# A four-layer fp32 model on one core: another order of the seven products of an expert slot, and the second ranking cut into ten parts

## The chip, the core and the metric

The kernel runs on one core of a Trainium2 chip. The core has TensorE (matrix products, PE in the profile), VectorE (DVE), ScalarE (ACT), GpSimd (POOL) and SyncE (SP, whose queue starts the loads). Each engine has its own program and runs it in order; the engines meet only in semaphores. The metric is the time of one execution on the device in microseconds.

## The reference, cut to what matters

Two layers, each a mixer and a feed-forward part with a residual and a layer norm behind it. 2048 tokens of width 512, everything in fp32. Layer 0 is a state-space mixer and a block-sparse feed-forward part, layer 1 is a linear attention and the mixture of experts in which the change lies:

```python
weights = _router_weights(x, Wr, temperature)          # sigmoid, exponentials, rank of 8 experts, top 2
gate = jnp.einsum('btd,edf->ebtf', x, Wg)               # 8 experts, 512 x 512
up = jnp.einsum('btd,edf->ebtf', x, Wu)
gate = gate.at[:NL].add(jnp.einsum('btd,edr,erf->ebtf', x, Ga, Gb))     # rank 64, 2 of the experts
up = up.at[:NL].add(jnp.einsum('btd,edr,erf->ebtf', x, Ua, Ub))
mid = jax.nn.silu(gate) * up
out = jnp.einsum('ebtf,efd->ebtd', mid, Wd)
out = out.at[:NL].add(jnp.einsum('ebtf,efr,erd->ebtd', mid[:NL], Da, Db))
return jnp.einsum('bte,ebtd->btd', weights, out)
```

## The kernel before

**Slots.** The experts' part runs in 32 slots. A slot is half an expert (256 of the 512 hidden columns) over half the tokens (1024); slots 0 to 15 take the first half of the tokens, 16 to 31 (`SLOTS` = 16) the second. Slots 18 to 29 are a loop, the others are written out. In a slot n TensorE makes the hidden sums of slot n (`up`) and, between them, the outputs of slot n-1 (`down`). fp32 products are made of three matmuls (`accumulate`, L1232: high x high, low x high, high x low), so every operand is there twice, as `_hi` (rounded, by ScalarE) and `_lo` (the rest, by VectorE or GpSimd).

**Seven products.** `up` doesn't make eight block products but seven of sums of blocks (Strassen's way in Winograd's form). Product q has an operand a[q] made of weights and b[q] made of tokens, and two halves i (gate and up), each of 6 matmuls of 512 columns. They go to three pairs of banks of PSUM: X (`attn_pvk`) takes q = 0, 2, 4, 6, one on top of the other, Y (`attn_pt`, `attn_pk`) takes q = 1, Z (`attn_po`) takes 3 and 5. Between them sums are read out: after q = 0 ScalarE copies X into c_t0 (`take`, semaphore s_e1) and VectorE adds Y to it (`combine`); after 2 and 4 ScalarE copies X again; after 3 and 5 VectorE adds Z. X after q = 6 is the last block (c_last): ScalarE takes silu of half 0 (L2300), VectorE multiplies half 1 by it (L2899). Only then may q = 0 of the next slot overwrite X: half 0 waits for the silu, half 1 for the product. q = 2 waits for the copies of s_e1.

**Down.** The eight `down` products c = 0 to 7 (6 matmuls each) go through a ring of two banks (`attn_pv`, `attn_pq`). VectorE adds each to `all_acc` with its router weight (`add_down`, L2762, in `turn`), which frees the bank. `downs(n)` places them: one after each of q = 0 to 3, two after 4, one after 5 and 6. Slots 3, 4, 7, 8 (`MERGING`) also put small matmuls of the rank-64 parts into the ring (L2478 to L2484; added by VectorE at L2773 and L2777), slot 10 (`TURNING`) transposes of the second half's tokens (L2493), slot 11 (`SCORING`) its router scores.

**Around it.** For slot n+1, ScalarE cuts a[q] (`up_high`) and VectorE makes the rest (`up_low`, L2720) while slot n runs; only q = 6 and the down weights (`down_high`, `down_low`, L2730) are made at the start of their own slot. GpSimd makes the sums of weights, the rest of the hidden values (`hidden_low`, L2020) and, in slot 15, four sums of tokens (`x_sums`, L2003 to L2013), from which b[q] of the second half is made: `x_high` on ScalarE, `x_low` (L2726) on VectorE, in slot 15 and at the start of slot 16. The ranking of the second half (`router(1, part)`) is in slot 12 (`RANKING`): part 0 after down product 0, 1 after 4, 2 after 6, 3 and 4 after 7, with two exponentials on ScalarE (`router_functions(1, 1)`) in front of the last silu. `side_work` calls them from `turn`. The weights that it makes are first used in slot 17. In slot 17 `finish` normalizes the first half's output.

The order within an engine is that in which `slot` of each engine is written; there is no scheduler.

## Time and profile before

| | us |
|---|---|
| median of 3 runs | 2319.34 (2316.86 to 2319.48) |
| the profiled execution | 2319.87, its span 2318.2 |
| TensorE busy in the span | 2257.0 |
| VectorE, ScalarE, GpSimd busy | 1582.3, 891.1, 766.6 |
| slots 0 to 31 | from about 1304 to 2300 of the span |

A row of busy time says how long an engine had an instruction in work; matmuls overlap, so their starts are the better measure. A row of the timeline ends in square brackets with the time the engine stood idle before it and the instruction whose end released it.

### The profile page before, as it was taken

The numbers are of one execution on the slowest core, as the hardware profiler recorded it, in microseconds if no ns is written. First come the engines' busy times: TensorE is split into PE (matmuls) and PEld (weight loads), VectorE is DVE, ScalarE is ACT, GpSimd is POOL, SyncE is SP. The second block draws the span as 40 slices with busy tenths as digits, with TensorE's granted clock in tenths as the row PEclk, the third lists the DMA queues.
The fourth block names the chain that finished last, engine by engine and source line by source line (L and its number), as shares of the span: only waits on it lengthen the run. The fifth ranks groups of instructions, "written<-read, shape, count | busy, mean of one in ns | idle before, by whom it ended". The sixth has DMA issues, their size and how long they took to land.

```text
span 2318.2 us, 30910 instructions
## 1 busy us (share of the span) xinstructions
PE 2257.0 (97%) x10746; PEld 1863.4 (80%) x10746; DVE 1582.3 (68%) x2394; ACT 891.1 (38%) x1455; POOL 766.6 (33%) x585
## 2 busy tenths in 40 slices
PE   8999999999999999999999899999999999999998
PEld 7887788888878888888877787878778778888886
DVE  5557777777778755683446776867677887666665
ACT  5456333333343222322232543534344444444443
POOL 0003544444413222342111523424233533333332
PEclk9999999999999999999999999999999999999999
DMA  6856222222150100000000122222011021111110
GB/s 210 230 153 185 64 73 72 72 72 72 55 200 15 37 19 19 23 1 19 1 1 28 64 73 91 73 82 82 28 55 55 28 91 55 54 54 54 54 36 37
DMA packets 93224, 155.95 MB, mean 67 GB/s; under 512 B 6576, under 2 KB 56752, under 8 KB 86848
## 3 DMA queue, kind: packets, MB, share of 16 engines
q1 hardware_dynamic: 93120, 154.59, 20.4%
q8 instruction: 61, 1.00, 0.2%
q14 instruction: 43, 0.35, 0.0%
HBM read 115.25 MB, written 39.32 MB: 67 GB/s over the span
## 4 chain that ended last, share of the span: by engine, by line
PE 62%; DVE 5%; issue 2%; ACT 1%; POOL 1%; DVEq 0%; POOLq 0%; ACTq 0%
PE attn_pvk L1235 4%; PE attn_pvk L1236 4%; PE attn_pvk L1237 4%; PE attn_pq L1235 2%; PE attn_pq L1236 2%; PE attn_pq L1237 2%; PE attn_po L1235 2%; PE attn_po L1236 2%; PE attn_po L1237 2%; PE attn_pv L1235 2%; PE attn_pv L1236 2%; PE attn_pv L1237 2%; PE attn_pv L85 2%; PE attn_pv L87 2%; PE attn_pv L86 2%
## 5 line engine op out<-in xcount | busy, mean ns | idle before, releaser
L2720 DVE TENSOR_TENSOR moe_a_lo<-moe_up_raw,moe_a_hi 128x512 fp32r<-128x512 f32 x192 | 183.3, 970 | 147.6 <-ACT moe_a_hi L2153 147.5
L2020 POOL TENSOR_TENSOR moe_h_lo<-moe_c_t,moe_h_hi 128x512 fp32r<-128x512 f32 x96 | 128.5, 1339 | 351.8 <-ACT moe_h_hi L2153 351.8
L1235 PE MATMUL attn_pvk<-moe_b_hi,moe_a_hi 128*128 128x512 f32 x512 | 201.5, 393 | 10.8 <-ACT moe_c_last L2300 7.0
L1237 PE MATMUL attn_pvk<-moe_b_hi,moe_a_lo 128*128 128x512 f32 x512 | 200.3, 391 | 0.0
L1236 PE MATMUL attn_pvk<-moe_b_lo,moe_a_hi 128*128 128x512 f32 x512 | 200.2, 391 | 0.0
L2153 ACT ACTIVATE moe_c_t<-attn_pvk 128x512 f32<-128x512 f32 x192 | 112.8, 595 | 175.9 <-PE attn_pvk L1237 174.1
L1349 POOL TENSOR_TENSOR ffn_h_lo<-ffn_h_f,ffn_h_hi 128x512 fp32r<-128x512 f32 x64 | 92.9, 1453 | 240.1 <-ACT ffn_h_hi L1416 240.1
L1593 DVE SCALAR_TENSOR_TENSOR all_acc<-attn_pvk,ffn_wts,all_acc 128x512 f32<-128x512 f32 x128 | 91.1, 749 | 93.3 <-PE attn_pvk L87 88.3
L2219 ACT ACTIVATE moe_c_t<-moe_c_t 128x512 f32<-128x512 f32 x96 | 60.4, 629 | 241.4 <-DVE moe_c_t L2802 241.3
L2153 ACT ACTIVATE moe_a_hi<-moe_up_raw 128x512 fp32r<-128x512 f32 x192 | 116.0, 624 | 56.4 <-POOL moe_up_raw L1990 56.4
L1235 PEld LDWEIGHTS attn_pvk<-moe_b_hi,moe_a_hi 128*128 128x128 f32 x512 | 96.6, 189 | 34.8 <-issue 8.9
L2762 DVE SCALAR_TENSOR_TENSOR all_acc<-attn_pv,moe_wts,all_acc 128x512 f32<-128x512 f32 x123 | 91.8, 746 | 37.7 <-PE attn_pv L1237 36.7
L1990 POOL TENSOR_TENSOR moe_up_raw<-moe_up_raw 128x512 f32<-128x512 f32 x32 | 52.0, 1624 | 188.2 <-DVE moe_a_lo L2720 188.1
L2802 DVE TENSOR_TENSOR moe_c_t<-moe_c_t,attn_po 128x512 f32<-128x512 f32 x128 | 86.3, 684 | 39.8 <-ACT moe_c_t L2153 36.5
L1178 DVE SCALAR_TENSOR_TENSOR mix_conv<-mix_acc,mix_cw,mix_conv 128x511 f32<-128x511 f32 (+2 forms) x96 | 71.8, 748 | 60.5 <-ACT mix_conv L686 58.2
L1237 PEld LDWEIGHTS attn_pvk<-moe_b_hi,moe_a_lo 128*128 128x128 f32 x512 | 96.7, 189 | 20.4
L2762 DVE SCALAR_TENSOR_TENSOR all_acc<-attn_pq,moe_wts,all_acc 128x512 f32<-128x512 f32 x133 | 99.1, 745 | 20.1 <-PE attn_pq L1237 17.1
L1236 PEld LDWEIGHTS attn_pvk<-moe_b_lo,moe_a_hi 128*128 128x128 f32 x512 | 96.7, 189 | 19.5
L1235 PE MATMUL attn_pq<-moe_dn_hi,moe_h_hi 128*128 128x512 f32 x266 | 105.5, 397 | 5.3 <-DVE all_acc L2762 4.0
L85 PE MATMUL mix_tp<-mix_wx_hi,mix_x 128*128 128x512 f32 x256 | 106.9, 417 | 0.0
L1235 PE MATMUL attn_po<-moe_b_hi,moe_a_hi 128*128 128x512 f32 x256 | 101.2, 395 | 4.0 <-DVE moe_c_t L2802 4.0
L85 PE MATMUL mix_acc<-mix_x_hi,mix_w_hi 128*128 128x512 f32 (+1 forms) x256 | 102.2, 399 | 1.7 <-DVE mix_x_lo L1153 0.9
(526 smaller groups left out, 6579.7 us busy)
## 6 DMA issues: line engine op xcount, KB each, us to landing
moe_up_raw<-in_e_up SPq DMA_DIRECT2D x28, 1024.0 KB, 6.1
moe_dn_raw<-in_e_dn SPq DMA_DIRECT2D x28, 512.0 KB, 3.7
xh<-mix_out_hi SPq DMA_DIRECT2D x32, 256.0 KB, 2.6
zs<-mix_out_z SPq DMA_DIRECT2D x32, 256.0 KB, 3.5
xl<-mix_out_lo SPq DMA_DIRECT2D x32, 256.0 KB, 3.9
mix_x<-xh SPq DMA_DIRECT2D x16, 512.0 KB, 4.1
mix_x<-xl SPq DMA_DIRECT2D x16, 512.0 KB, 5.2
mix_z_raw<-zs SPq DMA_DIRECT2D x16, 512.0 KB, 3.9
```

The source lines that it names most:

```text
L85: pe.matmul(out, lh, rh, start=first, stop=False)
L1178: nc.vector.scalar_tensor_tensor(out=conv[:, j % 2, d:SEQ], in0=acc[:, 2 * j % 4, 0:SEQ - d], scalar=cw[:, j, TAPS - 1 - d:TAPS - d], in1= ...
L1235: pe.matmul(out, lh, rh, start=first, stop=False, skip_group_check=True)
L1236: pe.matmul(out, lh, rl, start=False, stop=False, skip_group_check=True)
L1237: return pe.matmul(out, ll, rh, start=False, stop=True, skip_group_check=True)
L1349: nc.gpsimd.tensor_tensor(h_lo[:, f], h_f[:, f % 2], raw(h_hi[:, f]), ALU.subtract).then_inc(s_hlo, 1)
L1593: stt(out=acc[:, ch], in0=pd[c], scalar=wts[:, ch, bass.ds(F * u + f, 1)], in1=acc[:, ch], op0=ALU.mult, op1=ALU.add).then_inc(s_acc, 1)
L2020: tt(h_lo[:, m, tok], src, raw(h_hi[:, m, tok]), ALU.subtract).then_inc(s_hlo, 1)
L2153: copy = lambda out, src: nc.scalar.activation(out, src, ACT.Copy)
L2720: tt_(a_lo[q][:], src, raw(a_hi[q][:]), ALU.subtract).then_inc(s_alo, 1)
L2762: stt(out=acc[:, ch], in0=bank, scalar=wts[:, ch, w] if isinstance(w, slice) else wts[:, ch, bass.ds(w, 1)], in1=acc[:, ch], op0=ALU.mult, ...
L2802: tt_(c_t[tile][:, i], c_t[tile][:, i], bank(i), ALU.add).then_inc(sem, 1)
```

## The change

In every slot but slot 0 TensorE makes product 1 first and product 0 second; the down products keep their places (after the first, the second, and so on). `place_of` turns the waits on the count of products accordingly. ScalarE cuts a[6] and the down weights before it copies X for s_e1, where it did so after. The ranking of the second half is cut into ten parts: 0 and 1 stay in slot 12, 2 to 8 follow down products 1 to 7 of slot 13, part 9 down product 1 of slot 14; the two exponentials move to slot 13. The first half's ranking has the same instructions in the same order. Of the second half's token parts on VectorE, `x_low` 2 is made after the last product of slot 15 where 3 was, and 3, 5 and 6 within slot 16, after down products 0, 2 and 3. No instruction is added or removed.

```diff
+        TURN = (1, 0, 2, 3, 4, 5, 6)
...
+        place_of = lambda n, q: q if at(n, 0) else TURN[q]
...
-                reach(act, s_up, 14 * (n - 1) + 2 * q + 2)
+                reach(act, s_up, 14 * (n - 1) + 2 * place_of(n - 1, q) + 2)
...
-                    act.wait_ge(s_up, 14 * (SLOTS - 1) + 2 * q + 2)
+                    act.wait_ge(s_up, 14 * (SLOTS - 1) + 2 * place_of(SLOTS - 1, q) + 2)
...
-                act.wait_ge(s_up, 14 * n + 2 * q + i + 1)
+                act.wait_ge(s_up, 14 * n + 2 * place_of(n, q) + i + 1)
...
                     hidden_high(n - 1, (0, 1), used_by(n - 1, 7))
+                up_high(n, s, u, 6)
+                down_high(n, s)
                 if not at(n, 0):
                     take(n, 0, 0, s_e1, 0, 1)
                     take(n, 1, 0, s_e1, 0, 1)
+                lora_high(n, 0)
+                if at(n, SLOTS - 1):
+                    x_high(1, 0)
+                if at(n, RANKING + 1):
+                    router_functions(1, 1)
                 if at(n, SLOTS):
                     x_high(1, 5)
                     x_high(1, 6)
-                up_high(n, s, u, 6)
-                down_high(n, s)
-                lora_high(n, 0)
-                if at(n, SLOTS - 1):
-                    x_high(1, 0)
...
-                if at(n, RANKING):
-                    router_functions(1, 1)
...
-                for q in range(7):
+                for step in range(7):
+                    q = step if at(n, 0) else TURN[step]
                     for i in range(2):
                         if not (at(n, 0) and (q, i) in FIRST):
                             up(n, q, i)
-                    for c in downs(n)[q]:
+                    for c in downs(n)[step]:
                         extras(n, c)
...
                 if n == TOKENS_AT + 1:
-                    router(0, 2)
+                    for part in (2, 3, 4, 5):
+                        router(0, part)
                 if n == TOKENS_AT + 2:
-                    router(0, 3)
+                    router(0, 6)
+                    router(0, 7)
...
-                dve.wait_ge(s_up, 5 if at(n, 0) and (q, i) == (1, 1) else 14 * n + 2 * q + i + 1)
+                dve.wait_ge(s_up, 5 if at(n, 0) and (q, i) == (1, 1) else 14 * n + 2 * place_of(n, q) + i + 1)
...
-                    ranks(pr[:], cmp1, cmp2)
-                if part == 3:
+                if part in (2, 3, 4, 5):
+                    ranks(pr[:], cmp1, cmp2, part)
+                if part == 6:
                     link(red(sel[:], cmp1[:], AX_X, ALU.add))
                     ts(sel[:], sel[:], 1.5, None, ALU.is_lt).then_inc(s_router, 1)
                     dve.wait_ge(s_router, pair + 1)
                     link(tt_(sel[:], sel[:], pr[:], ALU.mult))
+                if part == 7:
                     inverse_of_sum(sel[:])
...
-                if at(n, RANKING):
-                    if c in (0, 4, 6, 7):
-                        router(1, {0: 0, 4: 1, 6: 2, 7: 3}[c])
-                    if c == 7:
-                        router(1, 4)
+                if at(n, RANKING) and c in (0, 4):
+                    router(1, c // 4)
+                if at(n, RANKING + 1) and c:
+                    router(1, c + 1)
+                if at(n, RANKING + 2) and c == 1:
+                    router(1, 9)
...
-                if at(n, SLOTS):
-                    x_low(1, 5)
-                    x_low(1, 6)
                 up_low(n, s, 6)
                 down_low(n, s)
                 turn(*order[0])
+                if at(n, SLOTS):
+                    x_low(1, 3)
...
                 turn(*order[2])
+                if at(n, SLOTS):
+                    x_low(1, 5)
...
                 turn(*order[3])
                 if more and not merging and not at(n, 0):
                     following(3)
+                if at(n, SLOTS):
+                    x_low(1, 6)
...
                 turn(*order[5])
-                if at(n, SLOTS - 1):
-                    x_low(1, 2)
...
                 if at(n, SLOTS - 1):
-                    x_low(1, 3)
+                    x_low(1, 2)
                 turn(*order[6])
```

TensorE at the seam of slots 15 and 16, the last three matmuls of down product 7 and the first three of slot 16. Before:

```order
L1235 MATMUL attn_pv<-moe_dn_hi_4439,moe_h_hi_4446 128x512
L1236 MATMUL attn_pv<-moe_dn_lo_4436,moe_h_hi_4446 128x512
L1237 MATMUL attn_pv<-moe_dn_hi_4439,moe_h_lo_4447 128x512
L1235 MATMUL attn_pvk<-moe_b_hi0_4422,moe_a_hi0_4415 128x512
L1236 MATMUL attn_pvk<-moe_b_lo0_4423,moe_a_hi0_4415 128x512
L1237 MATMUL attn_pvk<-moe_b_hi0_4422,moe_a_lo0_4461 128x512
```

Now:

```order
L1235 MATMUL attn_pv<-moe_dn_hi_4439,moe_h_hi_4446 128x512
L1236 MATMUL attn_pv<-moe_dn_lo_4436,moe_h_hi_4446 128x512
L1237 MATMUL attn_pv<-moe_dn_hi_4439,moe_h_lo_4447 128x512
L1235 MATMUL attn_pt<-moe_b_hi1_4424,moe_a_hi1_4416 128x512
L1236 MATMUL attn_pt<-moe_b_lo1_4425,moe_a_hi1_4416 128x512
L1237 MATMUL attn_pt<-moe_b_hi1_4424,moe_a_lo1_4462 128x512
```

The slot opens on the Y bank (`attn_pt`) with b[1], where it opened on X (`attn_pvk`) with b[0].

ScalarE at the start of slot 15 (every slot from 1 on has these rows; c_t2 and c_last are slot 14's hidden values). Before:

```order
L2153 ACTIVATE moe_h_hi_4446<-moe_c_t2_4448 128x512
L2153 ACTIVATE moe_h_hi_4446<-moe_c_last_4449 128x512
L2153 ACTIVATE moe_c_t0_4437<-attn_pvk 128x512 x2
L2153 ACTIVATE moe_a_hi6_4421<-moe_up_raw_4460 128x512
L2153 ACTIVATE moe_dn_hi_4439<-moe_dn_raw_4440 128x1024
```

Now:

```order
L2156 ACTIVATE moe_h_hi_4446<-moe_c_t2_4448 128x512
L2156 ACTIVATE moe_h_hi_4446<-moe_c_last_4449 128x512
L2156 ACTIVATE moe_a_hi6_4421<-moe_up_raw_4460 128x512
L2156 ACTIVATE moe_dn_hi_4439<-moe_dn_raw_4440 128x1024
L2156 ACTIVATE moe_c_t0_4437<-attn_pvk 128x512 x2
```

The two copies of X moved behind the cuts of a[6] and of the down weights.

VectorE from down product 6 of slot 15 to down product 0 of slot 16; b_lo2, b_lo3, b_lo5, b_lo6 are the token parts. Before:

```order
L2762 SCALAR_TENSOR_TENSOR all_acc_49<-attn_pq,moe_wts_4468,all_acc_49 128x512
L2726 TENSOR_TENSOR moe_b_lo2_4427<-moe_xr_4459,moe_b_hi2_4426 128x1024
L2720 TENSOR_TENSOR moe_a_lo5_4466<-moe_up_raw_4460,moe_a_hi5_4420 128x512
L2899 TENSOR_TENSOR moe_c_last_4449<-attn_pvk,moe_c_last_4449 128x512
L2726 TENSOR_TENSOR moe_b_lo3_4429<-moe_xr_4459,moe_b_hi3_4428 128x1024
L2762 SCALAR_TENSOR_TENSOR all_acc_49<-attn_pv,moe_wts_4468,all_acc_49 128x512
L2726 TENSOR_TENSOR moe_b_lo5_4433<-moe_xr_4459,moe_b_hi5_4432 128x1024
L2726 TENSOR_TENSOR moe_b_lo6_4435<-moe_xr_4459,moe_b_hi6_4434 128x1024
L2720 TENSOR_TENSOR moe_a_lo6_4467<-moe_up_raw_4460,moe_a_hi6_4421 128x512
L2730 TENSOR_TENSOR moe_dn_lo_4436<-moe_dn_raw_4440,moe_dn_hi_4439 128x1024
L2762 SCALAR_TENSOR_TENSOR all_acc_49<-attn_pq,moe_wts_4468,all_acc_49 128x512
```

Now:

```order
L2769 SCALAR_TENSOR_TENSOR all_acc_49<-attn_pq,moe_wts_4468,all_acc_49 128x512
L2727 TENSOR_TENSOR moe_a_lo5_4466<-moe_up_raw_4460,moe_a_hi5_4420 128x512
L2914 TENSOR_TENSOR moe_c_last_4449<-attn_pvk,moe_c_last_4449 128x512
L2733 TENSOR_TENSOR moe_b_lo2_4427<-moe_xr_4459,moe_b_hi2_4426 128x1024
L2769 SCALAR_TENSOR_TENSOR all_acc_49<-attn_pv,moe_wts_4468,all_acc_49 128x512
L2727 TENSOR_TENSOR moe_a_lo6_4467<-moe_up_raw_4460,moe_a_hi6_4421 128x512
L2737 TENSOR_TENSOR moe_dn_lo_4436<-moe_dn_raw_4440,moe_dn_hi_4439 128x1024
L2769 SCALAR_TENSOR_TENSOR all_acc_49<-attn_pq,moe_wts_4468,all_acc_49 128x512
L2733 TENSOR_TENSOR moe_b_lo3_4429<-moe_xr_4459,moe_b_hi3_4428 128x1024
```

Token part 2 moved behind c_last and stands alone before the add of down product 7; between that add and the next (down product 0) two token parts are gone.

## Rows read from the trace of the kernel before

**Rows 1.** The page's first part: busy us (share), instructions.
```profile
PE 2257.0 (97%) x10746; PEld 1863.4 (80%) x10746; DVE 1582.3 (68%) x2394; ACT 891.1 (38%) x1455; POOL 766.6 (33%) x585
```

**Rows 2.** Windows of slots 13, 16, 18, 19: length, busy PE PEld DVE ACT POOL, PEclk.
```profile
1713.28:1748.16 34.88, 30.77 (x133) 24.73 (x133) 30.37 (x53) 14.35 (x24) 10.61 (x8) 1.00 0.12 46
...
1808.08:1847.17 39.09, 33.65 (x134) 26.62 (x133) 32.91 (x33) 18.05 (x29) 21.20 (x11) 0.91 0.11 41
...
1877.24:1909.44 32.20, 30.50 (x133) 24.81 (x133) 26.13 (x31) 13.19 (x23) 12.43 (x9) 1.00 0.22 82
1909.44:1939.36 29.92, 29.92 (x133) 24.77 (x132) 20.71 (x26) 12.99 (x22) 10.98 (x8) 1.00 0.14 53
```

**Rows 3.** TensorE's waits in the slots: total us, times, longest.
```profile
PE attn_pvk L1235 <- ACT moe_c_last L2300: 7.0, 5, 2.5
...
PE attn_pq L1235 <- DVE all_acc L2762: 4.0, 4, 2.0
PE attn_pv L1235 <- DVE moe_up_raw L2773: 4.0, 4, 1.1
PE attn_pvk L1235 <- DVE moe_c_last L2899: 3.7, 3, 1.5
...
PE attn_pv L2493 <- DVE moe_xr L2786: 1.0, 2, 0.8
```

**Rows 4.** Timeline of ScalarE around the start of a slot of the loop.
```profile
2116.36 0.60 ACT L2300 ACTIVATE moe_c_last<-attn_pvk 128x512 f32<-128x512 f32 x1
...
2119.62 0.62 ACT L2153 ACTIVATE moe_h_hi<-moe_c_last 128x512 fp32r<-128x512 f32 x1
2120.52 0.60 ACT L2153 ACTIVATE moe_c_t<-attn_pvk 128x512 f32<-128x512 f32 x1 [0.28 <-PE attn_pvk L1237]
...
2122.30 0.62 ACT L2153 ACTIVATE moe_a_hi<-moe_up_raw 128x512 fp32r<-128x512 f32 x1
2122.82 1.05 ACT L2153 ACTIVATE moe_dn_hi<-moe_dn_raw 128x1024 fp32r<-128x1024 f32 x1
```

**Rows 5.** Timeline of TensorE, the first matmul after each of four stops.
```profile
1318.05 0.47 PE L1235 MATMUL attn_pvk<-moe_b_hi,moe_a_hi 128*128 128x512 f32 x1 [1.71 <-ACT moe_c_last L2300]
...
1449.30 0.47 PE L1235 MATMUL attn_pvk<-moe_b_hi,moe_a_hi 128*128 128x512 f32 x1 [0.88 <-ACT moe_c_last L2300]
...
1718.10 0.50 PE L1235 MATMUL attn_pvk<-moe_b_hi,moe_a_hi 128*128 128x512 f32 x1 [1.32 <-DVE moe_c_last L2899]
...
1728.99 0.50 PE L1235 MATMUL attn_pq<-moe_dn_hi,moe_h_hi 128*128 128x512 f32 x1 [1.08 <-DVE all_acc L2762]
```

**Rows 6.** Timeline of ScalarE, start of slot 1.
```profile
1319.43 0.63 ACT L2153 ACTIVATE moe_h_hi<-moe_c_last 128x512 fp32r<-128x512 f32 x1 [1.00 <-DVE moe_c_last L2899]
```

**Rows 7.** Timeline of VectorE, end of slot 12 and start of 13.
```profile
1714.17 0.69 DVE L2814 TENSOR_TENSOR moe_cmp<-moe_cmp,moe_lower 128x512 f32<-128x512 f32 x1
...
1721.69 1.02 DVE L2819 TENSOR_SCALAR moe_sum<-moe_sum 128x8 f32<-128x8 f32 x1
```

**Rows 8.** Timeline of VectorE, slot 3, a merged part.
```profile
1386.67 0.68 DVE L2773 TENSOR_TENSOR moe_up_raw<-attn_pv,moe_up_raw 128x512 f32<-128x512 f32 x1
```

**Rows 9.** Timeline of VectorE, seam of slots 15 and 16.
```profile
1811.05 2.85 DVE L2720 TENSOR_TENSOR moe_a_lo<-moe_up_raw,moe_a_hi 128x512 fp32r<-128x512 f32 x1
1813.83 0.68 DVE L2899 TENSOR_TENSOR moe_c_last<-attn_pvk,moe_c_last 128x512 f32<-128x512 f32 x1
1814.48 2.76 DVE L2726 TENSOR_TENSOR moe_b_lo<-moe_xr,moe_b_hi 128x1024 fp32r<-128x1024 f32 x1
```

**Rows 10.** Timeline of GpSimd at the same place.
```profile
1810.01 3.35 POOL L2009 TENSOR_TENSOR moe_xr<-moe_xr 128x1024 f32<-128x1024 f32 x1
1813.32 2.84 POOL L2013 TENSOR_TENSOR moe_xr<-moe_xr 128x1024 f32<-128x1024 f32 x1
```

**Rows 11.** Window of one of slot 16's two stretches at the lower clock.
```profile
1827.90:1831.30 3.40, 3.40 (x10) 2.63 (x9) 2.82 (x5) 1.68 (x4) 1.37 (x1) 0.50 0.88 360
```

**Rows 12.** The page's sixth part: the loads of down weights.
```profile
moe_dn_raw<-in_e_dn SPq DMA_DIRECT2D x28, 512.0 KB, 3.7
```

20 lines of the change are left out of this document (13 added, 7 removed).

## The prediction

> **What bounds the kernel now.** I read the page's first part, then windows cut at the slots, then TensorE's waits, and last the timelines of the engines around each stop. TensorE is busy for 2257.0 us of the span [rows 1], so only its stops can be won. Slot 19 lasts 29.92 us [rows 2]; it holds 14 half products and 8 down products, 22 sets of six matmuls, so a set takes 1.36 us. A slot of that length has no stop, and slots 19 to 31 all have it: there nothing can be won, only lost. The slots that are longer without extra matmuls are 13 (34.88), 16 (39.09) and 18 (32.20) [rows 2]. TensorE's waits in the slots are mostly for c_last: 7.0 us in 5 stops for its silu, 3.7 in 3 for its product [rows 3]. X of slot n can't be overwritten before both are read, and today q = 0, which overwrites it, comes first. The stops lie at the starts of slots 1, 5, 13, 16 and 18. The chip's clock is not what bounds these slots, but for two stretches of 3.4 us in slot 16 at 0.50 of full speed, 1.2 GHz [rows 11].
>
> **The seam of two slots, in a slot of the loop.** The silu of c_last starts at 2116.36 and takes 0.60. The copy at 2120.52 waited until 0.28 before its start for the first half of q = 0, so that half ran from 2118.88 to 2120.24: the room for the silu is 1.9 us [rows 4]. With q = 1 in front, q = 0 starts two sets later, and the room is 1.9 + 2.7 = 4.6 us. What pays is the copy of X for q = 2. Counted from the slot's start S, sets end at 1.36, 2.72 (q = 1), 4.08 (down 0), 5.44, 6.80 (q = 0), 8.16 (down 1), then comes q = 2. The first copy can start at S + 5.6 and ends by 6.3, where q = 2 wants it at 8.16: room 1.9 us, where it was five sets (6.8) less the copy. ScalarE must be free by then. Ahead of the copies stand the cuts of two hidden blocks, a[6] and the down weights: from about S + 0.2, 0.5 each for three and 1.05 for the last [rows 4], free at S + 2.8. So the loop keeps its 29.92, gain 0. VectorE gets a[6] and the down weights earlier and its two sums for c_t0 at about the same time as now (Y was late before, X is now).
>
> **Part by part, from slot 1 on.** A stop costs more than its idle time: slot 13 is 34.88 - 29.92 = 4.96 longer [rows 2], its three stops are idle for 1.71 (the same as slot 1's), 1.32 and 1.08 [rows 5]; the rest, 0.28 a stop, is the slow first matmuls. I add 0.28 to each.
>
> Slot 1: the stop of 1.71 [rows 5] goes, worth 2.0. Slot 1 has no down product before q = 2, so the copy has one set of room, not two. The hidden block from c_last is cut at 1319.43 [rows 6], then a[6] (0.5), down weights (1.0), copy (0.6) with 0.5 for the first [rows 4]: done at 1322.0. The slot now starts at about 1316.2, q = 2 wants it 5.44 later, 1321.6: 0.45 lost. Gain 1.5, bounds 0.5 (each step late by 0.3) and 2.0.
>
> Slots 3, 4, 7, 8: TensorE waits 4.0 in four stops for the merge of a rank-64 part [rows 3], because a bank isn't freed before VectorE has added it, behind its two sums for c_t0. The merge's add in slot 3 starts at 1386.67 [rows 8]. Now the second sum waits for the second copy of X: q = 0 ends at 1385.4, copy 0.6 with its releases 0.2 each, sum, next add at 1386.9. That is 0.2 later, and 0.1 in slots 4 and 8 where VectorE is late anyway: loss 0.6 in all, bounds 0 and 2.7 (four times one add of 0.68).
>
> Slot 5: the idle 0.88 [rows 5] goes, gain 1.16. Slot 10: the down weights are made 1.6 us earlier on VectorE, so that the bank of the first transposes is free in time: the longer of the two waits, 0.8 [rows 3], goes, gain 1.07.
>
> Slots 12 to 14: the four compares of 0.7 [rows 7] stood between down product 6 and a[5] of the next slot, the exponentials in front of the last silu, and parts 3 and 4 (7.7 us, one small step alone 1.02, held up by GpSimd [rows 7]) between down 7 and the add that frees the ring. In slot 13 they are one step behind each add. VectorE is busy for 20.7 us of a normal slot [rows 2]; parts 2 to 8 add about 7.5, and it ends below 29.92. The tightest place is the first sum for c_t2, wanted by q = 5 at S + 21.8: two parts of 0.7 stand before it, one of them behind GpSimd, and it comes at S + 20.2. After down 5 the delay is 1.4 us, and the new room at the seam is 4.6. ScalarE's exponentials and two table loads lie before the silu of c_t0, which nobody needs for 5 us. Nothing is late: the whole 4.96 goes. Bounds 3.0 (the third stop's kind returns once or twice) and 4.96.
>
> Slot 18: both stops (slot 17's `finish` puts normalizing steps before a[5]) lie at the seam, at most 1.5 long and so inside 2.7: 32.20 - 29.92, gain 2.28.
>
> Slot 16, the uncertain one. At its start GpSimd makes two sums of tokens, 1810.01 and 1813.32 [rows 10]. VectorE's a[5] starts at 1811.05 and ends 0.54 after the first of them; the token part at 1814.48 ends 1.08 after the second [rows 9, 10]: an instruction of VectorE with both operands in SBUF waits until GpSimd's is done, and GpSimd's second in turn took 2.26 from the end of a[5]. The product of c_last, with one operand in PSUM, takes 0.68 [rows 9]. I replay the new order with these prices, from the slot's start S. First sum S + 2.2 to 4.5, a[5] to 5.1, c_last to 5.7; q = 0 wants it at 5.44: 0.3 lost. Second sum to 7.3, token part 2 to 8.4, add of down 7 to 9.1; down 1 wants that bank at 7.1: 2.0 lost, a new stop. Then a[6] 10.3, down weights 12.7, add of down 0 13.4 (wanted 13.2: 0.2), token part 3 15.1 (wanted 14.8: 0.3), two sums and an add 16.9, gate, a[0], a[1], add 19.8, token part 5 21.6, a[2] 23.4, add of down 3 24.1 (wanted 23.3: 0.8), a[3], token part 6, sum for c_t2 27.0 (wanted 25.5: 1.6). Lost 5.2 where 9.17 are lost now, gain 4.0. The lower clock isn't in the 5.2: both drops followed stops of 2.0 and 2.5 us [rows 3, 11], the pair of 1.7 and 1.3 in slot 13 brought none [rows 2]; the new stop of 2.0 lies between. A drop would cost 3.4 x 0.5 = 1.7. Bounds 0 and 9.17.
>
> **The sum.** 1.5 - 0.6 + 1.16 + 1.07 + 4.96 + 2.28 + 4.0 = 14.4. Against the profiled execution, 2319.87, that gives 2305.5; it lies 0.5 above the median of the runs, and I leave that as room for a drop of the clock that I don't expect.
>
> **Rivals.** *The stops of slot 16 only change place*: GpSimd and VectorE hold each other up as long as now, or two drops of the clock remain. Its VectorE is busy for 32.91 of 39.09 us [rows 2], which speaks for it, and the token parts are spread among seven GpSimd instructions; against it, the stop for down 2 falls from 2.0 to 0.2 by order alone. Gain 10.4, with a drop or worse merges less: 2308.5 to 2311.5.
>
> *Token part 2 gets in ahead of GpSimd's second sum.* It is ready 0.6 us behind a[5], and the sum is queued already, which speaks against it. If it is first, it ends at S + 6.8, the add of down 7 at 7.5, and the stop of 2.0 shrinks to 0.4: 2302.5, and with the rest of the slot easing 2300.5. The Trainium skill ("SBUF — State Buffer", Who interferes with whom) says of this pair that whoever issues first has the shared port for the whole instruction, whatever its shape. By that rule this rival hangs on 0.6 us of order alone; the trace agrees with the lock, by the 0.54 and 1.08 above.
>
> *The loop pays.* The down weights' cut now stands ahead of the copies, and it waits for their load: a late load would hold up q = 2 in every slot. A load lands 3.7 us after its issue [rows 12] and is issued some 20 us ahead. It decides once ScalarE is free later than S + 4.7 (2.8 + 1.9). To eat the gain of 14.4 and 4.6 more, 31 slots must each lose 0.61, ScalarE free at S + 5.3, 2.5 us later than the rows show: 2324 or more.
>
> *Gains come back elsewhere*: a stop whose place I don't see, in the merged slots or through VectorE in slots 13 and 14: 2311.5 to 2320.
>
> **Chances.** About 0.2% (4.6 us) can be told from no change. Forecast 0.60 (2303 to 2308.5), slot 16 unchanged 0.15, part 2 first 0.12, gains given back 0.08, the loop pays 0.05. Faster by over 0.2% (below 2314.7) holds the first three and a third of the fourth, 0.89; same 0.06; slower 0.05. The range 2300.5 to 2311.5 holds the first three but for their edges.
>
> **What would show it.** Slots of the loop stay at 29.92; c_last no longer releases TensorE but once, in slot 16; slots 13, 14 and 18 last 29.92 to 30.1; in slot 1 a stop of about 0.4 for the copy of X; merged parts hold TensorE for 4.5 where it was 4.0; slot 16 lasts 35, with its longest stop in front of down 1. Wrong I'd be if any slot of the loop is longer, or if slot 16 keeps 39.

## The result and the profile after

The changed kernel takes 2303.5 us in the median of 4 runs (2302.83 to 2307.83), the kernel before 2319.22 beside it. The ratio is 0.9943, with a 95% interval of 0.9931 to 0.9954: faster by 0.57%. The profiled execution took 2302.83, 17.0 less than that of before. A second series of the unaltered changed kernel, five runs, gave 2304.16 against 2316.24, ratio 0.9947 [0.9933, 0.9961]. From series to series the kernel before moves by up to 3 us (medians of 2316.24 to 2319.22), the changed kernel by 0.7 in its two, so medians are compared inside one series below, and where they cross a series, slot by slot in the traces as well. All durations in the text are us.

Windows of the trace of after, cut at the slots: 13, 15, 16, 17 and 18, a slot of the loop, and a stretch inside slot 16. Columns: stretch, length, busy PE, PEld, DVE, ACT, POOL, granted clock of TensorE (share of 2.4 GHz), DMA share, GB/s. They answer to [rows 2] and [rows 11].

```profile
1708.52:1738.44 29.92, 29.92 (x134) 24.77 (x133) 24.77 (x37) 15.62 (x26) 12.34 (x8) 1.00 0.15 53
1768.36:1798.70 30.34, 30.18 (x134) 24.70 (x133) 24.10 (x27) 13.97 (x22) 16.93 (x9) 1.00 0.14 52
1798.70:1832.58 33.88, 32.13 (x133) 25.76 (x132) 31.23 (x33) 17.95 (x29) 21.40 (x11) 0.95 0.12 47
1832.58:1862.50 29.92, 29.92 (x133) 24.77 (x132) 27.08 (x47) 12.88 (x22) 14.94 (x11) 1.00 0.26 98
1862.50:1892.42 29.92, 29.92 (x133) 24.77 (x132) 24.43 (x30) 13.03 (x22) 11.37 (x8) 1.00 0.22 80
1807.68:1812.10 4.42, 4.42 (x12) 3.50 (x13) 4.42 (x4) 1.83 (x2) 4.34 (x4) 0.61 0.05 13
...
2131.78:2161.70 29.92, 29.92 (x133) 24.77 (x132) 20.55 (x26) 12.89 (x22) 12.08 (x8) 1.00 0.14 53
```

Slots 13 and 18, 34.88 and 32.20 before, are 29.92 now. Slot 16 went from 39.09 to 33.88 and still has a stretch at 1.2 GHz. Slot 15 got longer, by 0.34; the only others are merged ones, slots 3 and 7, by 0.17 and 0.14. The loop kept its 29.92.

TensorE's waits in the slots, after (total, times, longest), beside [rows 3]:

```profile
PE attn_pv L1235 <- DVE moe_up_raw L2780: 4.3, 4, 1.1
PE attn_po L1235 <- DVE moe_c_t L2809: 4.2, 2, 4.1
PE attn_pv L1235 <- DVE all_acc L2769: 1.8, 1, 1.8
...
PE attn_pq L1235 <- DVE all_acc L2769: 1.0, 2, 0.5
PE attn_pv L2496 <- DVE moe_xr L2793: 0.2, 1, 0.2
```

`c_last`, which released TensorE in eight stops (10.7) before, is gone from the list. (In slot 16 it still costs 0.2, too short for the list: the second half of product 0 starts at S + 5.56, just behind VectorE's c_last, and its first matmuls stand 0.35 and 0.34 apart instead of 0.23. S is always the start of the slot.) The one new line is the third: down product 1 of slot 16 waits 1.8 for the add of down product 7. (The 4.1 in the second line lies in slot 0, in front of product 5, and is as it was.)

ScalarE at the start of a slot of the loop that begins at 2131.78, after, beside [rows 4]. Columns: start, duration, engine, line, operation, out<-in; in brackets the idle time before it and what ended it.

```profile
2133.56 1.05 ACT L2156 ACTIVATE moe_dn_hi<-moe_dn_raw 128x1024 fp32r<-128x1024 f32 x1
2137.42 0.60 ACT L2156 ACTIVATE moe_c_t<-attn_pvk 128x512 f32<-128x512 f32 x1 [2.81 <-PE attn_pvk L1237]
```

ScalarE is free at S + 2.8 and stands idle until the first half of product 0 is done; its copy starts at S + 5.64. The prediction had 2.8 and 5.6.

### The profile page after: what moved, and what is told of

Read it like the earlier page. It is cut to its first block, busy times and chain, and to the rows that moved or that the text cites. A ratio compares the mean times of both kernels' runs of the same rounds, so it can differ in the third digit from the quotient of the medians.

```text
span 2301.1 us, 30912 instructions
## 1 busy us (share of the span) xinstructions
PE 2252.3 (98%) x10746; PEld 1863.0 (81%) x10746; DVE 1582.4 (69%) x2394; ACT 890.3 (39%) x1455; POOL 792.8 (34%) x585
## 4 chain that ended last, share of the span: by engine, by line
PE 65%; DVE 3%; issue 1%; POOL 0%; ACT 0%; POOLq 0%; DVEq 0%; ACTq 0%
PE attn_pvk L1235 5%; PE attn_pvk L1236 5%; PE attn_pvk L1237 5%; PE attn_pq L1235 3%; PE attn_po L1235 2%; PE attn_po L1236 2%; PE attn_po L1237 2%; PE attn_pq L1236 2%; PE attn_pq L1237 2%; PE attn_pv L1235 2%; PE attn_pv L1236 2%; PE attn_pv L1237 2%; PE attn_pv L85 2%; PE attn_pv L87 2%; PE attn_pv L86 2%
## 5 line engine op out<-in xcount | busy, mean ns | idle before, releaser
L2727 DVE TENSOR_TENSOR moe_a_lo<-moe_up_raw,moe_a_hi 128x512 fp32r<-128x512 f32 x192 | 173.3, 919 | 102.4 <-ACT moe_a_hi L2156 102.3
L2769 DVE SCALAR_TENSOR_TENSOR all_acc<-attn_pv,moe_wts,all_acc 128x512 f32<-128x512 f32 x123 | 91.9, 747 | 37.3 <-PE attn_pv L1237 34.3
L1235 PEld LDWEIGHTS attn_pvk<-moe_b_hi,moe_a_hi 128*128 128x128 f32 x512 | 96.8, 189 | 20.7 <-DVE moe_c_last L2914 0.4
L459 POOL TENSOR_TENSOR mix_pre<-mix_xf,mix_heads 128x1024 f32<-128x1024 f32 x16 | 47.1, 2947 | 167.9 <-ACT mix_xf L568 167.9
```

What stands on the lines that cost most here:

```text
L1235: pe.matmul(out, lh, rh, start=first, stop=False, skip_group_check=True)
L2727: tt_(a_lo[q][:], src, raw(a_hi[q][:]), ALU.subtract).then_inc(s_alo, 1)
L2769: stt(out=acc[:, ch], in0=bank, scalar=wts[:, ch, w] if isinstance(w, slice) else wts[:, ch, bass.ds(w, 1)], in1=acc[:, ch], op0=ALU.mult, ...
```

## The experiments

Twelve runs; one of them is the changed kernel again, unaltered. The first three take the change apart: each is the kernel before with one of its three parts.

### One part alone

**order_alone**: the order of the products, with ScalarE's copies behind its cuts.

```diff
+        TURN = (1, 0, 2, 3, 4, 5, 6)
...
+                    q = step if at(n, 0) else TURN[step]
```

> The kernel before with one part of the change: product 1 ahead of product 0 in slots 1 to 31, and ScalarE's cuts of a[6] and of the down weights ahead of its copies of X. The ranking and the token parts stand as before. My theory: the stops for c_last at the starts of slots 1, 5, 13 and 18 go (1.9 + 1.2 + 3.3 + 2.3), the wait of slot 10 shrinks (1.2), the third stop of slot 13 stays, for an add of VectorE (1.1 to 1.4), the merges lose 0.2 to 0.6, and slot 16 keeps about 39 because VectorE has the same rows in the same order there: 0 to 1 gained. Sum 9 to 10, some 2309.5, slots of the loop 29.92. Rival (ranking and token parts bring most of it, order alone little): 2314 to 2319.

Measured: 2315.05 against 2317.74, ratio 0.9986 [0.9977, 0.9995]. That is 2.7 won where I expected 9 to 10. By slots it wins 3.7. Slots 1, 5, 10 and 18 behave as expected, slot 16 too (39.23), but slot 13 is *longer* than before. Windows of slots 13 and 16, and of a stretch in 13:

```profile
1707.92:1745.16 37.24, 32.54 (x133) 26.36 (x132) 30.59 (x53) 14.34 (x24) 10.64 (x8) 0.91 0.12 43
1805.43:1844.66 39.23, 32.42 (x133) 25.67 (x132) 32.11 (x33) 17.94 (x29) 20.76 (x11) 0.96 0.11 41
...
1724.25:1728.95 4.70, 4.70 (x13) 3.68 (x12) 3.76 (x6) 2.72 (x6) 1.65 (x2) 0.54 0.79 321
```

VectorE and TensorE at the place, timelines of the same kernel:

```profile
1712.62 0.74 DVE L2765 SCALAR_TENSOR_TENSOR all_acc<-attn_pv,moe_wts,all_acc 128x512 f32<-128x512 f32 x1
1713.28 0.67 DVE L2849 TENSOR_REDUCE moe_sel<-moe_cmp 128x64 f32<-128x512 f32 x1
...
1722.86 0.74 DVE L2765 SCALAR_TENSOR_TENSOR all_acc<-attn_pq,moe_wts,all_acc 128x512 f32<-128x512 f32 x1
...
1723.66 0.80 PE L1235 MATMUL attn_pq<-moe_dn_hi,moe_h_hi 128*128 128x512 f32 x1 [4.70 <-DVE all_acc L2765]
```

The first row is the add of down product 7, the second the start of the rest of the ranking (until 1721.08), the third the add of down product 0, for whose bank down product 2 waits 4.70. That matmul starts at S + 15.74 (1723.66 - 1707.92). In the kernel before the same matmul started at 1728.99 [rows 5] in the slot of 1713.28 [rows 2]: S + 15.71. **The order of the products did not move it at all.** VectorE's chain through the ranking ends when it ends. Before, TensorE spent the time in three stops (1.71, 1.32, 1.08); with the new order the first two are gone and all of it lies in one of 4.70, behind which twelve matmuls ran 0.43 apart instead of 0.23, at 1.2 GHz: 2.3 more. So slot 13 lost 7.3 where it had lost 5.0. My expectation had credited the order with the stops that it removes, and had not asked what stands behind them in VectorE's queue. Slot 16 of this kernel shows the same: down product 2 starts at S + 18.5, where it started at S + 18.3 before. In front of it TensorE now stops for 1.0, 1.7 and 4.1, before it was 2.5, 0.9 and 2.0. Behind the middle one the clock stayed full (matmuls 0.23 apart):

```profile
1815.39 0.50 PE L1235 MATMUL attn_pv<-moe_dn_hi,moe_h_hi 128*128 128x512 f32 x1 [1.74 <-DVE all_acc L2765]
```

**ranking_alone**: only the ranking in ten parts.

```diff
+                if at(n, RANKING) and c in (0, 4):
+                    router(1, c // 4)
+                if at(n, RANKING + 1) and c:
+                    router(1, c + 1)
```

> The kernel before with one other part of the change: the second half's ranking in ten parts over slots 12, 13 and 14, its two exponentials in slot 13. Products, copies and token parts as before. My theory: all three stops of slot 13 go, 4 to 5 us, some 2314.7, and nothing else moves; so this part and the order both claim the 3.3 of slot 13's first two stops, and the parts alone add up to more than the change. If the sum for c_last comes late behind a part of the ranking, a stop of 0.5 to 1 stands at the start of slot 14, because the old order has 1.9 of room there: 2315.5. Rival (the ranking only matters together with the new order): 2317 to 2319.

Measured: 2313.67 against 2317.74, ratio 0.9981 [0.9972, 0.9990], 4.1 won. Windows of slots 13 and 14:

```profile
1711.78:1741.70 29.92, 29.92 (x133) 24.78 (x132) 25.05 (x37) 15.86 (x26) 11.25 (x8) 1.00 0.14 53
1741.70:1771.90 30.20, 30.20 (x134) 24.70 (x133) 25.96 (x43) 12.86 (x22) 10.33 (x8) 1.00 0.14 53
```

All three stops of slot 13 go, and a trace of one comes back at the start of slot 14, where the old order had little room. It costs 0.28; the place was expected, the size was taken as 0.5 to 1.

**tokens_alone**: only token parts 2, 3, 5 and 6 at their new places.

```diff
                 if at(n, SLOTS - 1):
-                    x_low(1, 3)
+                    x_low(1, 2)
                 turn(*order[6])
```

> The kernel before with the third part of the change: token part 2 of the second half behind the last product of slot 15, parts 3, 5 and 6 within slot 16. Products, copies and ranking as before. My theory: the two stops for c_last at the start of slot 16 stay (2.5 and 0.9), since the silu waits for ScalarE's own queue and the product for VectorE's a[5] beside GpSimd; the stop of 2.0 in front of down 2 goes, with its drop of the clock: 3.5 to 4 gained, some 2315.5, slot 16 about 35. Rival (VectorE's work in slot 16, 32.9 us of it, is the bound whatever its order): slot 16 stays above 38, 2318 to 2319.5.

Measured: 2315.11 against 2317.74, ratio 0.9987 [0.9978, 0.9996], 2.6 won. Slot 16 and TensorE's waits in it:

```profile
1806.18:1842.31 36.13, 30.73 (x133) 24.74 (x133) 31.83 (x33) 18.09 (x29) 20.16 (x11) 1.00 0.12 44
```
```profile
PE attn_pvk L1235 <- ACT moe_c_last L2300: 2.6, 1, 2.6
PE attn_po L1235 <- DVE moe_c_t L2802: 1.7, 1, 1.7
PE attn_pvk L1235 <- DVE moe_c_last L2899: 1.2, 1, 1.2
```

The two stops for c_last stay, the stop in front of down 2 is gone with its drop of the clock, as expected. Not expected: the other drop, behind the stop of 2.5 for c_last, is gone too, although that stop is still there (2.6), and there is a stop of 1.7 in front of product 5, for a sum of c_t2 (L2802). Slot 16 is 36.1, not 35.

The three parts alone win 2.7 + 4.1 + 2.6 = 9.4 between medians; together they win 12 to 15.7. By the slots of the traces it is 3.7 + 4.7 + 3.0 = 11.3 against 16.5. The whole is more than the parts.

**order_and_ranking**: two of the three parts, without the token parts.

> The kernel before with the order of products, the copies and the ranking as changed, and the token parts as before. My theory: the parts of the change need each other. The order alone moves slot 13's stop to the add of down product 0 behind the ranking (37.24), the ranking in ten parts takes it away there (29.92, 7.3 won on top of the order's 2.7), and slot 16 keeps the 39.2 that the order alone has: 2308 to 2309. The token parts are then worth 5 with the new order, where they were worth 2.6 alone. Rival (the interplay lies between order and token parts only, the ranking is worth 4.1 with any order): 2311.

Measured, in the series of the repeated changed kernel: 2308.73 against 2316.24, ratio 0.9969 [0.9957, 0.9981]; the changed kernel beside it 2304.16. Windows of slots 13 and 16:

```profile
1708.03:1737.95 29.92, 29.92 (x134) 24.77 (x133) 24.77 (x37) 15.63 (x26) 12.37 (x8) 1.00 0.14 53
1798.23:1837.46 39.23, 32.43 (x134) 25.67 (x132) 32.06 (x33) 17.95 (x29) 20.76 (x11) 0.96 0.11 41
```

Slot 13 falls from 37.24 to 29.92 by the ranking: 7.3 with the new order, 5.0 with the old one. Slot 16 keeps the 39.23 of the order alone, and the token parts bring it to 33.9: 5.3, against 3.0 with the old order. Between the medians the token parts are worth 4.6. This settles where the interplay lies. In slot 13 the ranking in ten parts does the work: without the new order it also gives 29.92. There the order alone costs 2.4, and with the ranking it costs nothing and adds the 0.3 of slot 14. In slot 16 the order alone gives nothing (39.23 against 39.09), and behind the moved token parts it gives 2.25 (36.13 to 33.88). In both slots it does no good as long as VectorE's queue behind c_last is long.

### The room for the copies

**copies_first**: the changed kernel with ScalarE's copies of X ahead of its cuts again.

```diff
-                up_high(n, s, u, 6)
-                down_high(n, s)
                 if not at(n, 0):
                     take(n, 0, 0, s_e1, 0, 1)
                     take(n, 1, 0, s_e1, 0, 1)
+                up_high(n, s, u, 6)
+                down_high(n, s)
```

> The changed kernel with one part undone: ScalarE copies X (for product 2) ahead of its cuts of a[6] and of the down weights, as it did before the change. With product 0 second, the copies come at S + 5.6 and S + 6.9 (S: start of the slot), the cuts behind them end at S + 9.1, VectorE's rests of a[6] and the down weights at S + 11, the add of down product 0 at S + 11.7, where down product 2 wants its bank at S + 10.9. My theory: about 0.8 and 0.28 lost in each of some 30 slots, every slot of the loop 31.0 instead of 29.92: 2330 to 2337, slower than before. Rival (the two banks of the ring have room for it): the loop stays 29.92 and the time within 1 us of 2303.5.

Measured: 2351.03 against 2317.74, ratio 1.0148 [1.0133, 1.0164]; some 47.5 slower than the changed kernel (across series; the spans of the two traces differ by 47.8). The direction was right, the places were not. Windows of slot 3 and of a slot of the loop, and the matmul behind slot 3's longest stop:

```profile
1374.46:1415.68 41.22, 36.50 (x153) 29.58 (x152) 21.54 (x30) 10.89 (x19) 10.22 (x8) 0.92 0.20 77
2057.06:2087.29 30.23, 30.23 (x133) 24.70 (x132) 19.04 (x26) 12.78 (x22) 10.64 (x8) 1.00 0.14 52
```
```profile
1385.93 0.58 PE L2481 MATMUL attn_pv<-lora_r,lora_l 128*128 128x256 f32 x1 [4.01 <-DVE moe_up_raw L2780]
```

A slot of the loop loses 0.31, not 1.1: the add of down 0 starts at S + 10.2 and not at 11.7, because VectorE's rest of the down weights took 1.23 there, not held up by GpSimd, where it takes 2.13 in the loop of the changed kernel. Half of the loss lies in slots 3, 4, 7 and 8, some 6 each: there the ring of two banks carries the merged parts too, and the first of them waits 4.0 for an add that stands behind the cuts. Slots 10 and 11, which put transposes and router scores into the same ring, lose 5.5 and 5.8 in the same way, with one stop of 4.0 each:

```profile
1642.25 1.12 PE L2496 MATMUL attn_pv<-ident,all_acc 128*128 128x128 f32 x4 [4.01 <-DVE moe_xr L2793]
```

Moving the cuts ahead of the copies is thus no detail of the change but a condition for it, and it is the slots with more in the ring that need it most.

### Slot 16

**changed_again**: the changed kernel, unaltered. **merge_early**: in the merged slots the two adds between the two sums for c_t0; the code of slot 16 is that of the changed kernel.

```diff
-                        extras(n, c)
+                        if not (merging and c == 1):
+                            extras(n, c)
...
                 combine(n, 0, 0, Y, 1, s_e1, s_c11)
+                if merging:
+                    extras(n, 1)
                 combine(n, 1, 0, Y, 1, s_e1, s_c11)
```

> The changed kernel once more, unaltered, beside the others of this call. Its first profile has slot 16 at 33.89 with the clock at half speed for some 4 us behind the stop in front of down 1 and no stop in front of product 5; the kernel with early merges has the same code in slot 16 and shows 34.83, with the clock full and a stop of 1.9 in front of product 5. My theory: both are executions of one kernel, the drop of the clock and the later stop take each other's place because VectorE's chain ends at the same time or 1.2 later (when GpSimd gets in ahead of a[3]). So slot 16 shows one of the two again, 33.9 or 34.8, and slot 1 29.92 or 30.6; median 2302.5 to 2304. Rival (the early merges themselves cost slot 16 0.9): 33.9 again with a drop.

> The changed kernel with one thing moved in slots 3, 4, 7 and 8 on VectorE: the two adds of the merged parts that stand behind the second sum for c_t0 come between the first sum and the second. Theory: the second sum waits 0.67 us for ScalarE's second copy of X, and the merge behind it holds its bank as long; with the adds in that gap down product 1 gets its bank 0.6 to 0.9 earlier, each stop of 1.1 falls to 0.4, 2.4 to 2.8 won in four slots, some 2300.7; slots 3 and 7 last 34.1. Rival (the merge's matmuls end too late for the gap, the ring of two banks is the bound): the adds wait for TensorE, the stop keeps 0.9 or more and the sum behind them comes later: within 1 us of the changed kernel.

Measured: merge_early 2300.70 against 2317.88, ratio 0.9929 [0.9915, 0.9942]. Its slots 3, 4, 7 and 8 are 34.03, 34.77, 34.09 and 34.81, where the changed kernel has 34.80, 35.54, 34.77 and 35.49: 2.9 won, 0.7 a slot. The first matmul of down product 1 in slot 3, in the changed kernel and in merge_early:

```profile
1385.02 0.50 PE L1235 MATMUL attn_pv<-moe_dn_hi,moe_h_hi 128*128 128x512 f32 x1 [1.06 <-DVE moe_up_raw L2780]
```
```profile
1384.49 0.50 PE L1235 MATMUL attn_pv<-moe_dn_hi,moe_h_hi 128*128 128x512 f32 x1 [0.31 <-DVE moe_up_raw L2780]
```

And slot 16, first in changed_again (whole, and the stretch behind the stop), then in merge_early (the same):

```profile
1800.81:1834.67 33.86, 32.11 (x134) 25.73 (x132) 31.21 (x33) 17.95 (x29) 21.43 (x11) 0.95 0.13 47
1809.79:1814.20 4.41, 4.41 (x12) 3.49 (x13) 4.41 (x4) 1.84 (x2) 4.34 (x3) 0.61 0.06 13
```
```profile
1796.00:1830.83 34.83, 31.17 (x134) 24.39 (x132) 32.19 (x33) 17.84 (x29) 21.13 (x11) 1.00 0.13 46
...
1804.98:1810.00 5.02, 5.02 (x22) 4.19 (x23) 5.02 (x4) 1.85 (x2) 4.94 (x4) 1.00 0.15 37
```

The same stop of 1.75 stands in front of down 1 in all three executions. In after and changed_again the clock falls behind it; in merge_early it doesn't, and then TensorE, sooner at the next places, waits 0.2 in front of down 5 and 1.7 in front of product 5. The repeated kernel came out as my theory and its rival (the early merges themselves cost slot 16 0.9) both allow, so it doesn't decide between them. What speaks for the theory are order_alone and order_and_ranking: they have no early merges, the same stop of 1.74 stands in front of down 1 of their slot 16, and the clock stayed full behind it both times. That the same kernel can give both forms is not shown.

**add7_first**: the add of down 7 ahead of token part 2. **sum2_later**: GpSimd's last sum of tokens behind its rests of the hidden blocks.

```diff
+                turn(*order[6])
                 if at(n, SLOTS - 1):
                     x_low(1, 2)
-                turn(*order[6])
```

```diff
                     x_sums(1, 2)
-                    x_sums(1, 3)
...
                     hidden_low(n - 1, (0, 1))
+                if at(n, SLOTS):
+                    x_sums(1, 3)
```

> The changed kernel with one thing turned round: at the seam of slots 15 and 16 VectorE adds down product 7 before it makes token part 2, where it does so after. S is the start of slot 16. Theory A (VectorE's chain up to the add of down product 0 is the bound): the add of down 7 ends at S + 6.1, so the stop of 1.8 in front of down 1 goes; token part 2, a[6], the down weights and the add of down 0 follow as before and end at S + 12.8, where down 2 now wants its bank at S + 11.0: a new stop of about 1.8 in front of down 2, slot 16 still 33.5 to 34, the time within 1 us of the changed kernel's (about 2303). Theory B (the stop and the drop of the clock behind it are a cost by themselves): nothing else is late, 1.9 + 0.3 + 1.7 are won, slot 16 30.0 to 30.5, some 2299.5.

> The changed kernel with one thing moved on GpSimd: the last sum of tokens (2.9 us beside VectorE) from the end of slot 15 to behind the rests of the hidden blocks at the start of slot 16. It makes what the prediction's rival on the shared port supposed: token part 2 is not held up by that sum. GpSimd is idle from S + 4.3 until ScalarE's cut at S + 6.0, so token part 2 runs from S + 5.4 in 1.2 instead of 2.8, the add of down 7 ends at S + 7.2 and the stop of 1.9 in front of down 1 falls to 0.1. Theory: VectorE's chain is only 1.6 shorter, a[6], the down weights and the add of down 0 end at S + 11.2 to 12 (wanted 11.0), a stop of 0.3 to 1.2 in front of down 2 and one of 0.5 to 1.5 in front of product 5; slot 16 31.5 to 33, 1 to 2.5 won: 2301 to 2302.5. Rival (the sum collides just as long with the down weights' rest, since somebody must wait): slot 16 33.5 or more, 2303 to 2304.

Measured: add7_first 2304.07 against 2317.88, ratio 0.9940 [0.9927, 0.9954], no gain, and its slot 16 lasts 34.8, where theory A had 33.5 to 34 and theory B 30 to 30.5. sum2_later 2302.57 against 2316.24, ratio 0.9940 [0.9926, 0.9953], 1.6 below the changed kernel of its series with ranges that overlap. TensorE's stops in slot 16, add7_first (S = 1797.54), then sum2_later (S = 1799.66):

```profile
1810.44 0.50 PE L1235 MATMUL attn_pq<-moe_dn_hi,moe_h_hi 128*128 128x512 f32 x1 [1.31 <-DVE all_acc L2769]
...
1824.04 0.47 PE L1235 MATMUL attn_po<-moe_b_hi,moe_a_hi 128*128 128x512 f32 x1 [1.70 <-DVE moe_c_t L2809]
```
```profile
1813.69 0.47 PE L1235 MATMUL attn_po<-moe_b_hi,moe_a_hi 128*128 128x512 f32 x1 [0.96 <-issue]
1822.53 0.50 PE L1235 MATMUL attn_pv<-moe_dn_hi,moe_h_hi 128*128 128x512 f32 x1 [0.40 <-DVE all_acc L2770]
1825.71 0.47 PE L1235 MATMUL attn_po<-moe_b_hi,moe_a_hi 128*128 128x512 f32 x1 [1.53 <-DVE moe_c_t L2810]
```

Both took the stop in front of down 1 away (0.3 is left of it in sum2_later), and both lost it again further on. Product 5 starts at S + 26.5 in add7_first, S + 26.5 in merge_early (1822.54 - 1796.00) and S + 26.1 in sum2_later. What stands in front of it decides, and that is VectorE's whole chain up to the sum for c_t2. Token part 2 in the changed kernel, then token parts 2 and 3 in sum2_later:

```profile
1804.13 2.83 DVE L2733 TENSOR_TENSOR moe_b_lo<-moe_xr,moe_b_hi 128x1024 fp32r<-128x1024 f32 x1
```

```profile
1805.09 1.21 DVE L2734 TENSOR_TENSOR moe_b_lo<-moe_xr,moe_b_hi 128x1024 fp32r<-128x1024 f32 x1
...
1810.83 2.76 DVE L2734 TENSOR_TENSOR moe_b_lo<-moe_xr,moe_b_hi 128x1024 fp32r<-128x1024 f32 x1
```

Part 2 fell from 2.83 to 1.21 as expected, but the moved sum met part 3 instead, which took 1.64 in the changed kernel. The range given for its slot 16 (31.5 to 33) was missed: it is 34.3, longer than the changed kernel's 33.9, so the 1.6 between the medians isn't a gain that its trace shows.

**slot16_spread** makes VectorE's chain up to that sum shorter: add of down 7 first, the rest of the down weights behind down 4 and 5, token part 6 behind the sums. **all_moves** adds the early merges and, in slot 15, a[3] behind the sums. **all_moves_2** puts a[3] behind them in slot 16 as well, and in slot 1 the copies ahead of the cut of the down weights.

```diff
                 up_low(n, s, 6)
-                down_low(n, s)
+                if not at(n, SLOTS):
+                    down_low(n, s)
                 turn(*order[0])
...
                 turn(*order[4])
+                if at(n, SLOTS):
+                    down_low(n, s)
```

```diff
-                if more and not merging and not at(n, 0):
+                if more and not merging and not at(n, 0, SLOTS - 1, SLOTS):
                     following(3)
-                if at(n, SLOTS):
-                    x_low(1, 6)
                 combine(n, 0, 2, Z, 3, s_u4, s_c22)
                 combine(n, 1, 2, Z, 3, s_u4, s_c22)
+                if at(n, SLOTS - 1, SLOTS):
+                    following(3)
+                if at(n, SLOTS):
+                    x_low(1, 6)
```

> The changed kernel with three things moved in slot 16 on VectorE: the add of down product 7 ahead of token part 2, the rest of the down weights (2.3 us) from the slot's start to behind down products 4 and 5, token part 6 behind the two sums for c_t2. By theory A of the run before (VectorE's order, not its total of 31.2 us, is the bound): add of down 7 at S + 6.1, token part 2 by 8.2, a[6] 9.3, add of down 0 10.0 (wanted 11.0), token part 3 11.7 (12.4), the first sum for c_t2 by 21.3 (21.9), the add of down 4 by 24.0 (24.6): no stop over 0.3, slot 16 30.1 to 30.5, 3.5 won, some 2299.7. Rival (VectorE's total is the bound, since 31.2 us of work don't fit into 29.92): the stops come back before product 5, down 6 or at the start of slot 17, slots 16 and 17 together over 62.

> The three moves in slot 16, the early merges, and one more in slot 15: the two sums for c_t2 ahead of a[3] of slot 16, which GpSimd's sum of tokens holds up for 2.2 us. Theory: the gains lie in different slots and add up: 3.5 + 2.6 + 0.4 = 6.5, some 2296.7, slot 15 back at 29.92. Rival (gains of neighbouring slots overlap, or the drops of the clock change place): 2299 to 2301.

> The five moves of the run with all of them, and two more: a[3] of slot 17 behind the two sums for c_t2 in slot 16 as well, and in slot 1 ScalarE's copies of X ahead of its cut of the down weights. In the run before, GpSimd's rest of a hidden block started 0.03 us ahead of a[3], a[3] took 1.80 where it took 0.68, and product 5 waited 0.9 for the sum behind it; with the sums in front, which read PSUM and are not held up, that stop goes (1.2 with its slow matmuls). The stop of 0.4 in slot 1 for the copy goes (0.7). Theory: slot 16 30.5 to 30.8 whoever comes first, slot 1 29.92, median 2295.5 to 2296.5. Rival (a drop of the clock or a wait elsewhere takes them back): 2297.5 to 2298.5.

Measured: slot16_spread 2300.97 against 2317.88, ratio 0.9932 [0.9918, 0.9945]; all_moves 2297.82, 0.9914 [0.9901, 0.9928]; all_moves_2 2294.71 against 2316.24, 0.9910 [0.9894, 0.9925], and 9.4 below the changed kernel of its series (2294.19 to 2296.63 against 2303.24 to 2304.91). all_moves misses its 2296.7 by 1.1, of which 0.9 is explained below; its slot 15 is back at 29.92 as expected. all_moves_2 came out 0.8 better than its 2295.5 to 2296.5. Slot 16 in the three:

```profile
1795.83:1826.63 30.80, 30.76 (x134) 24.54 (x132) 28.71 (x31) 17.31 (x29) 19.96 (x11) 1.00 0.11 41
```
```profile
1795.97:1827.70 31.73, 30.93 (x133) 24.46 (x132) 29.74 (x31) 17.12 (x28) 19.29 (x11) 1.00 0.11 37
```
```profile
1793.20:1823.93 30.73, 30.65 (x133) 24.54 (x132) 28.63 (x31) 17.23 (x29) 19.42 (x11) 1.00 0.11 41
```

The stops didn't come back, as theory A said: slots 16 and 17 of slot16_spread take 60.7 together, where the rival had over 62. Slot 16 is a little above the 30.1 to 30.5 expected. But order and total aren't cleanly apart in this run: VectorE's busy time in slot 16 fell from 31.2 to 28.7. Of these 2.5, 1.45 stand in slot 17 instead (27.1 to 28.5), and 1.1 are gone from both: the rest of the down weights takes 1.21 at its new place, where it took 2.30 beside GpSimd. The 0.9 between the first two windows is one meeting. VectorE's a[3] and GpSimd's rest of a hidden block, in slot16_spread, then in all_moves:

```profile
1816.84 0.68 DVE L2727 TENSOR_TENSOR moe_a_lo<-moe_s,moe_a_hi 128x512 fp32r<-128x512 f32 x1
...
1816.82 1.85 POOL L2023 TENSOR_TENSOR moe_h_lo<-moe_c_t,moe_h_hi 128x512 fp32r<-128x512 f32 x1 [1.12 <-ACT moe_h_hi L2156]
```
```profile
1816.88 1.80 DVE L2727 TENSOR_TENSOR moe_a_lo<-moe_s,moe_a_hi 128x512 fp32r<-128x512 f32 x1
...
1816.85 1.28 POOL L2023 TENSOR_TENSOR moe_h_lo<-moe_c_t,moe_h_hi 128x512 fp32r<-128x512 f32 x1 [1.10 <-ACT moe_h_hi L2156]
```

They start within 0.03 of each other both times, GpSimd's first by the profile. Once VectorE runs in its 0.68 and GpSimd takes 1.85 instead of 1.3, once GpSimd runs in 1.28 and VectorE takes 1.80. The Trainium skill ("SBUF — State Buffer", Who interferes with whom) says that the one that issues first has the shared port for the whole instruction and the other blocks fully. These rows agree that one of the two runs undisturbed and the other waits, with 0.6 lost on one side or 1.1 on the other; which of them issued first can't be read off starts this close. In merge_early, where GpSimd's started 0.19 ahead, a[3] took 1.63. In all_moves_2 the sums for c_t2, which read PSUM, stand in front: GpSimd's instruction started 0.06 ahead of them and took 1.30, the two sums took 1.27 together, and slot 16 has 30.73. That it no longer matters who is first is what this one execution suggests; the other order wasn't seen.

## Why the prediction came out as it did

Forecast 2305.5, measured 2303.5; the range of 2300.5 to 2311.5 holds it. The second series has 2304.16, which lies in it too. Against the profiled execution of before the forecast was a gain of 14.4; the medians give 15.7 in one series and 12.1 in the other, and the forecast lies between them. By its own steps, in the two profiled executions:

| step | predicted | measured |
|---|---|---|
| slot 1 | 1.5 | 2.0 |
| merged slots 3, 4, 7, 8 | -0.6 | -0.2 |
| slot 5 | 1.16 | 1.17 |
| slot 10 | 1.07 | 1.25 |
| slots 12 to 14 | 4.96 | 4.96 |
| slot 15 | 0 | -0.34 |
| slot 16 | 4.0 | 5.2 |
| slots 17, 18 | 2.28 | 2.43 |
| up to slot 1 | 0 | 0.5 |
| sum | 14.4 | 17.0 |

Slot lengths of before come from the starts of its slots, in the way of [rows 2]. The last 0.5 is luck: the code up to there is the same, and the start of slot 1 varies between 1312.8 and 1317.7 in the traces of kernels that share it.

**The loop** is right in every number: room for the copies, ScalarE free at S + 2.8, 29.92. copies_first shows what the condition is worth.

**Slot 1.** The stop of 0.4 for the copy isn't in the trace of after. It is in those of add7_first, merge_early, all_moves and sum2_later, which have the same code there. In add7_first:

```profile
1319.91 0.47 PE L1235 MATMUL attn_pvk<-moe_b_hi,moe_a_hi 128*128 128x512 f32 x1 [0.40 <-ACT moe_c_t L2156]
```

What goes with it is the clock in slot 0. Behind its stop of 4.1, which both kernels have, the clock stays at 1.2 GHz for some 5.0 in after and 3.3 in add7_first:

```profile
1308.16:1313.16 5.00, 5.00 (x13) 3.90 (x12) 4.49 (x5) 2.56 (x5) 2.47 (x2) 0.52 0.25 58
```
```profile
1307.21:1310.49 3.28, 3.28 (x9) 2.56 (x8) 2.64 (x3) 2.70 (x5) 2.57 (x2) 0.52 0.37 88
```

When TensorE is late by the clock it doesn't wait for the copy; when the clock is back sooner, it does. All nine traces with this code in slot 1 fit: eleven or more matmuls at the lower clock and no stop in five (after, changed_again, order_alone, order_and_ranking, slot16_spread), eight at most and the stop in four. From the restart in slot 0 to the end of slot 1 it is 38.0 in after and 37.8 in add7_first, so the stop takes back most of what the clock gave. The copy's lateness was forecast rightly, its price was not: a stop of 0.4 makes slot 1 30.6, so 0.7 with the slow first matmuls that the forecast added to every other stop; it had 0.45.

**The merges** hold TensorE for 4.3 (4.0 before, 4.5 predicted). The mechanism was right, the size a bit too large. merge_early shows that part of the wait was a matter of order too: 2.9 can be had.

**Slots 12 to 14** came out to the hundredth. The prediction doesn't say which part does what: the ranking in ten parts brings 4.7 of the 4.96 by itself, the order the last 0.3, in slot 14. order_alone is the run where that mattered, and my own expectation of it was off by 7. One term was too large: parts 2 to 8 of the ranking add 4.1 to VectorE's busy time (24.77 in slot 13 against 20.7), not 7.5.

**Slot 16.** The new stop in front of down 1 is 1.75 idle (2.0 with its first matmuls), forecast 2.0. The replay of VectorE beside GpSimd was close: a[5] ends at S + 4.9 (forecast 5.1), token part 2 at 8.3 (8.4), the add of down 7 at 8.9 (9.1), the add of down 0 at 12.8 (13.4). Two steps failed in the executions of the changed kernel. The forecast called a drop of the clock one "that I don't expect", and there is one, 1.7 lost. And the later stops that it counted, 2.9 in all (0.2, 0.3, 0.8 and 1.6), are not there, since TensorE comes later by that drop and a[3] did not meet GpSimd. In merge_early, with the clock full, they are there: 0.1 in front of product 3, 0.4 in front of down 5, 1.9 in front of product 5, each as the distance between two matmuls beyond the usual one, and its slot 16 is 34.8, where the forecast said 35. The two forms differ by 1.0, and the forecast priced the drop as coming on top of the stops. In the executions at hand it comes in their place, and that two errors of 1.7 and 2.9 partly cancel is luck: the 5.2 won here would have been 4.3 in the other form.

**Slot 15**, where the forecast saw no change, lost 0.34. VectorE, where the sum for c_t2 stands behind a[3], and GpSimd:

```profile
1787.47 2.22 DVE L2727 TENSOR_TENSOR moe_a_lo<-moe_s,moe_a_hi 128x512 fp32r<-128x512 f32 x1
...
1786.29 2.85 POOL L2006 TENSOR_TENSOR moe_xr<-moe_xr 128x1024 f32<-128x1024 f32 x1
```

a[3] takes 2.22 because GpSimd's sum of tokens, started 1.2 earlier, runs until 1789.1. It took 2.23 before as well. New is that the sum of tokens starts at S + 17.9, where it started at S + 17.6, and product 5 has no room for that. ranking_alone and tokens_alone keep the slot as it was, order_alone and order_and_ranking have 30.35: it is a price of the new order. With the sums in front (all_moves and all_moves_2) slot 15 is 29.92.

**The rivals.** That slot 16's stops only change place didn't happen as a whole; but it is what add7_first and sum2_later did with the one that was left. With token part 2 behind c_last, it never got in ahead of GpSimd's second sum in any trace. sum2_later forced it, and the gain of 3 to 5 that the rival promised did not come: the stop in front of down 1 fell to 0.3 (it said 0.4), and "the rest of the slot easing" was its wrong half. The loop paid nothing, and but for the 0.2 of the merged slots no gain came back there or in slots 13 and 14.

## What to carry to other kernels

A stop that one wait ends hides the next wait in the same queue: before crediting an edit with a stop, write down when the late engine gets to the work behind it, counted from the slot's start. If that time is the same with the edit, the stops only join, and one long stop can be dearer than three short ones, by the clock. Where two engines share a port, put instructions that read PSUM in front of those that can be held up. Here that won 0.4 in slot 15 and took a stop out of slot 16 that was there in one trace and not in another.

## What the runs showed of the hardware

- Two instructions of VectorE and GpSimd that start within 0.03 of each other change who pays: 0.68 and 1.85, or 1.80 and 1.28. Kernels that differ elsewhere can so differ by 0.9 in a slot.
- A wait too short for the list of waits still costs: in the loop of copies_first two matmuls stand 0.39 and 0.34 apart instead of 0.23. VectorE's add ends at S + 11.0, the bank is wanted at S + 10.9, so a bank late by about 0.1 costs 0.3 a slot, 30.23 instead of 29.92.
- The stop of 1.75 in front of down 1 of slot 16 was followed by some 4.4 with a mean clock of 0.61 in two executions (after, changed_again) and by full clock in three (merge_early, and at 1.74 in order_alone and order_and_ranking). The stop of 2.5 to 2.6 for c_last at the start of slot 16 was followed by the lower clock in the kernel before and in ranking_alone, and by full clock in tokens_alone. The stops of 4.0 and more (slot 0, slot 16 of order_alone and order_and_ranking, slot 13 of order_alone, slots 3, 10 and 11 of copies_first) all brought a drop. Whether one follows a stop of 1.7 to 2.6 I can't forecast from these runs; that stays open.
